# First attention's output stage: two normalisation chains laid between one another on the vector engine, the group loop written out, and the matrix engine's order rewritten to match

## The reference, cut to what matters

```python
attn_out = ctx @ out_w + out_b
h = _ln(x + attn_out, ln1_g, ln1_b)
ffn = jax.nn.gelu(h @ ffn_w1 + ffn_b1, approximate=False) @ ffn_w2 + ffn_b2
return _ln(h + ffn, ln2_g, ln2_b)
```

## Time and profile before

| | us |
|---|---|
| median of 3 runs | 3836.94 |
| the runs | 3833.84 to 3843.2 |
| the profiled execution, its own time | 3845.26 |
| its span, first to last instruction | 3843.5 |
| mean granted PE clock in it | 0.898 of full |
| the changed stage, from its first DVE operation to its last | 923.50 to 1095.64 |
| PE busy over the whole span | 3181.4 (83%) |
| DVE busy over the whole span | 2368.5 (62%) |

### The profile page before, as it was taken

How to read it: one execution, slowest core, us unless ns; L and a number is a source line. 1 busy time by engine, 2 the same in 40 slices (tenths; PEclk the granted TensorE clock), 3 DMA queues, 4 the chain that set the end, 5 groups by cost and what they waited for, 6 DMA issues and landing times. The chain is left out here.

```text
span 3843.5 us, 68233 instructions
## 1 busy us (share of the span) xinstructions
PE 3181.4 (83%) x25621; PEld 1748.6 (45%) x25621; DVE 2368.5 (62%) x5084; ACT 1844.5 (48%) x3309; POOL 921.2 (24%) x732
## 2 busy tenths in 40 slices
PE   5748888885759999797699969998888888889899
PEld 2213333331337655573222227763555444555676
DVE  5457777772656455564599942236778777778322
ACT  3214555553226423363289925434555555555444
POOL 1007888894100223000000000001121112212100
PEclk8668999997879899896599969998999988999999
DMA  4112323221033000132422210028444335432100
GB/s 146 41 51 72 106 76 103 79 91 31 12 93 132 2 1 1 45 133 79 144 58 67 68 35 1 1 81 219 122 122 101 108 103 128 122 103 82 31 9 12
DMA packets 229588, 289.46 MB, mean 75 GB/s; under 512 B 44861, under 2 KB 164121, under 8 KB 226950
## 3 DMA queue, kind: packets, MB, share of 16 engines
q1 hardware_dynamic: 229303, 285.61, 25.0%
HBM read 229.49 MB, written 56.55 MB: 74 GB/s over the span
## 5 line engine op out<-in xcount | busy, mean ns | idle before, releaser
L1169 POOL TENSOR_TENSOR l0aa_e<-l0aa_e,l0aa_et 128x512 f32<-128x512 f32 x432 | 538.1, 1274 | 139.1 <-ACT l0aa_e L1311 139.1
L2407 ACT ACTIVATE l1ba_sg<-l1ba_sg,l1ba_mn 128x128 f32<-128x128 f32 (+7 forms) x512 | 394.1, 771 | 303.4 <-DVE l1ba_mn L2451 302.4
L2451 DVE CUSTOM_DVE_ANT_0 l1ba_sg<-l1ba_pS,l1ba_tab 128x128 f32<-128x128 f32 (+7 forms) x512 | 369.0, 745 | 167.4 <-PE l1ba_pS L2347 90.1
L2347 PE MATMUL l1ba_pS<-l1b_k,l1ba_qs 64*128 64x448 f32 (+7 forms) x2048 | 372.2, 470 | 103.5 <-DMA l1ba_qs<-l1b_qd 64.9
L1342 DVE TENSOR_REDUCE l0aa_low<-l0aa_pP 128x8 f32<-128x1024 f32 x288 | 342.2, 1220 | 164.4 <-PE l0aa_pP L1193 163.6
L2460 DVE STREAM_TRANSPOSE l1ba_pT<-l1ba_sg 128x1024 f32<-128x1024 f32 (+3 forms) x344 | 367.1, 1067 | 35.7 <-PE l1ba_pO L2367 32.3
L1311 ACT ACTIVATE l0aa_e<-l0aa_pS 128x512 f32<-128x512 f32 x432 | 257.0, 595 | 259.5 <-PE l0aa_pS L1226 152.7
L2367 PE MATMUL l1ba_pO<-l1ba_pT,l1ba_v 32*64 32x256 f32 x9216 | 324.0, 397 | 5.5 <-ACT l1ba_y L2422 4.6
L319 PEld LDWEIGHTS f_pY<-l_w,f_hT 128*128 128x128 f32 x2048 | 268.1, 192 | 123.8 <-issue 118.8
L2314 POOL TENSOR_TENSOR l1ba_co<-l1ba_co,l1ba_rb 128x1024 f32<-128x1024 f32 x64 | 151.1, 2360 | 709.6 <-ACT l1ba_co L2415 676.7
L2817 ACT ACTIVATE l1aa_e<-l1aa_e 128x1536 f32<-128x1536 f32 x192 | 284.6, 1484 | 43.2 <-DVE l1aa_e L2858 25.9
(11 more groups left out here) (398 smaller groups left out, 5008.1 us busy)
## 6 DMA issues: line engine op xcount, KB each, us to landing
f_wB<-l0f_weights SPq DMA_DIRECT2D x16, 2048.0 KB, 7.2
l1ba_qs<-l1b_qd SPq DMA_DIRECT2D x128, 256.0 KB
l1ba_tab<-l1b_table SPq DMA_DIRECT2D x64, 512.0 KB
l1ba_rb<-l1b_rdd SPq DMA_DIRECT2D x64, 512.0 KB
l0aa_et<-l0a_table SPq DMA_DIRECT2D x16, 1536.0 KB
l1b_qd<-l1bp_part SPq DMA_DIRECT2D x64, 256.0 KB, 2.3
l0aa_et<-l0a_table SPq DMA_DIRECT2D x16, 512.0 KB
l0aa_qs<-l0a_qd SPq DMA_DIRECT2D x64, 96.0 KB
```

Of the source, the lines that this page charges most:

```text
L1169: nc.gpsimd.tensor_tensor(es, es, t, ALU.mult).then_inc(multiplied, 1)
L2347: ins = nc.tensor.matmul(pS[n % 2][:, at:at + half], qs[lo:lo + HALF, r % 2, i + k, :], ks[lo:lo + HALF, key:key + half], start=True, stop ...
L2407: nc.scalar.activation(row, row, ACT.Exp, bias=mn[:, r % 2, i + k:i + k + 1], scale=-1.0, accum_out=den[:, r % 2, i + k:i + k + 1]).then_i ...
L2451: nc.vector.tensor_tensor_reduce(row, scores, bias, 1.0, 3e38, ALU.add, ALU.min, mn[:, r % 2, h:h + 1]).then_inc(m_done, 1)
```

## The change

The loop over pairs of groups is gone: all engines' instructions are written out for eight groups, and register arithmetic on semaphore values falls away. On DVE the sequence is cut into pieces (`sum_B`, `projected`, `ln_newton`, `sum_A`, `apply_B`, `finish_A`, `take_sums`, `finish_B`), and in turn `g` the pieces of chain B of group g-1 stand between those of chain A of group g+1. PE's order is rewritten: `pB` of group g-1 now stands behind `pT` of group g, `pA` of g+1 ahead of the hidden tiles, `pR` of g+1 between the second and third hidden tile, `pC` of g+2 behind the fourth. Some waits are added that the new order needs (`rB_in`, `h_ready`, `a_done`, `f_in`). The arithmetic is the same.

```diff
-            def make_h(g, par):
-
-                steps = Steps(dve, stA, A_STEPS, g)
-                dve.wait_ge(cg_in[par], (g // 2 + 1) * 32)
-                dve.wait_ge(c_done, g + 1)
-                nc.vector.tensor_tensor(cT[:], cg[:, par, :], pC[:], ALU.mult).then_inc(c_in, 1)
+            def take_sums(g):
+
+                if g < GROUPS:
+                    dve.wait_ge(cg_in[g % 2], (g // 2 + 1) * 32)
+                    dve.wait_ge(c_done, g + 1)
+                    if g:
+                        dve.wait_ge(a_done, g)
+                    nc.vector.tensor_tensor(cT[:], cg[:, g % 2, :], pC[:], ALU.mult).then_inc(c_in, 1)
...
             dve.wait_ge(w_in, 16 * NW)
-            make_h(0, 0)
-            groups(dve, step)
+            take_sums(0)
+            for g in range(-1, GROUPS + 1):
+                steps_A, steps_B = Steps(dve, stA, LN_STEPS + 3, g + 1), Steps(dve, stB, LN_STEPS + 3, g - 1)
+                if g >= 1:
+                    sum_B(g - 1, steps_B)
+                if g + 1 < GROUPS:
+                    projected(g + 1)
+                if g >= 1:
+                    ln_newton(nc, dve, SB, steps_B, roughB, g)
+                if g + 1 < GROUPS:
+                    sum_A(g + 1, steps_A)
+                if g >= 1:
+                    apply_B(steps_B)
+                if g + 1 < GROUPS:
+                    finish_A(g + 1, steps_A)
+                take_sums(g + 2)
+                if g >= 1:
+                    finish_B(g - 1, steps_B)
...
-            divisors(0, 0)
+            divisors(0)
             project(0)
+            divisors(1)
             turn_back(0)
-            groups(pe, step)
+            for g in range(GROUPS):
+                turn(g)
+                if g:
+                    turn_sums(g - 1)
+                project(g + 1)
+                hidden(g, 0)
+                hidden(g, 1)
+                turn_back(g + 1)
+                hidden(g, 2)
+                hidden(g, 3)
+                divisors(g + 2)
+                back(g)
+            turn_sums(GROUPS - 1)
```

More of the change, by code:

```diff
@@ L1863, in power @@
             def power(S, ve, rough, g):
[L1864 to L1873, removed]
+                if 0 <= g < GROUPS:
+                    pool.wait_ge(ve, g + 1)
+                    nc.gpsimd.tensor_tensor(S["y"][:], S["ve"][:], C["mhalf"][:, 0:GROUP_BLOCKS], ALU.pow).then_inc(rough, 1)
+            for g in range(-1, GROUPS + 1):
+                power(SB, veB, roughB, g - 1)
+                power(SA, veA, roughA, g + 1)
         @block.vector
@@ L1889, in make_h, with statistics, projected, sum_A @@
+            def statistics(src, S, steps, ve_ready):
+                for k in range(GROUP_BLOCKS):
+                    ins = nc.vector.bn_stats(S["st"][:, k, :], src[:, k, :])
+                steps.done(ins)
+                ln_variance(nc, S, steps, ve_ready)
+            def projected(g):
                 dve.wait_ge(a_done, g + 1)
+                if g:
+                    dve.wait_ge(aB_done, g)
                 nc.vector.tensor_tensor(blocks(aT), blocks(pA), spread(ob), ALU.add).then_inc(a_in, 1)
+            def sum_A(g, steps):
@@ L1894, in make_h, with sum_B @@
                 steps.done(nc.vector.tensor_tensor(uA[:], uA[:], spread(g1), ALU.mult))
-                nc.vector.tensor_tensor(h[:, par], uA[:], spread(c1), ALU.add).then_inc(h_ready, 1)
+                if g >= 2:
+                    dve.wait_ge(rB_in, g - 1)
+                nc.vector.tensor_tensor(h[:, g % 2], uA[:], spread(c1), ALU.add).then_inc(h_ready, 1)
                 steps.close()
[L1898 to L1902, removed]
+            def sum_B(g, steps):
@@ L1938, in project, with divisors @@
-            def project(g):
-                pe.wait_ge(c_in, g + 3)
-                for k in range(GROUP_BLOCKS):
[L1941 to L1952, removed]
-                ins.then_inc(hT_done, 1)
[L1954 to L1962, removed]
+            def divisors(g):
+                if g < GROUPS:
+                    pe.wait_ge(cg_in[g % 2], (g // 2 + 1) * 32)
+                    if g:
+                        pe.wait_ge(c_in, g)
+                    nc.tensor.matmul(pC[:], sel[:], dn[:, g % 2, :], start=True, stop=True).then_inc(c_done, 1)
@@ new lines, in project, with turn_back @@
+            def project(g):
+                if g < GROUPS:
+                    pe.wait_ge(c_in, g + 1)
+                    if g:
+                        pe.wait_ge(a_in, g)
+                    for k in range(GROUP_BLOCKS):
+                        ins = nc.tensor.matmul(pA[:, k * P:(k + 1) * P], cT[:, (3 - k) * P:(4 - k) * P], ow[:], start=True, stop=True)
+                    ins.then_inc(a_done, 1)
+            def turn_back(g):
+                if g < GROUPS:
+                    pe.wait_ge(a_in, g + 1)
+                    if g:
+                        pe.wait_ge(h_ready, g)
+                    nc.tensor.matmul(pR[:], C["flip"][:], aT[:], start=True, stop=True).then_inc(aB_done, 1)
@@ L1963, in step, with back @@
+            def back(g):
+                if g:
+                    pe.wait_ge(f_in, g)
                 for t in range(FT):
```

76 lines of the change are left out of this document (48 added, 28 removed).

## The result

| us | before | changed |
|---|---|---|
| first measurement, median (lowest to highest), 5 runs each | 3836.94 (3833.84 to 3846.44) | 3812.47 (3805.96 to 3815.93) |
| second measurement, 17 and 6 runs | 3844.65 (3831.68 to 3859.51) | 3807.93 (3795.46 to 3812.67) |
| profiled execution, its span | 3843.5 | 3810.6 |
| stage, first `pC` on PE to the next stage's first product | 169.4 | 134.3 |
| stage, reciprocals to the last sum into `x` | 172.1 | 136.8 |

The ratio is 0.9928, with a 95% interval of 0.9909 to 0.9947, in the first measurement, and 0.9896 (0.9871 to 0.9921) in the second: 24.5 and 36.7 us faster. The forecast was 3806 (3797 to 3821), 31 faster, a ratio of 0.9919. Both measured times lie in that range, and both intervals hold that ratio; neither gain lies in the narrower 28 to 35 that the prediction named for its main case.

A forecast was written before the change was run, and what follows sets the result against it. A chain going back and forth between PE and DVE was taken as the bound. Turns of 13.9 instead of 18.6, with start and tail, gave 33.5 saved; less 2.5 for clock dips, 31, so 3806 us, range 3797 to 3821.

The forecast's parts named there:

- main case: Whole program: the forecast of 28 to 35 us saved, chance 0.57.
- the four waits: DVE's turn: idle 1.12 for POOL in chain B, 1.25 for `pA`, 1.35 for `pR`, 1.12 for POOL in chain A.
- The turn, 13.9: DVE's middle turn, `rB` to `rB`, in its new order: 13.9 us in place of 18.6.
- `pR` binds `rA` by 0.13: DVE's middle turn: `rA` can start only at 4.27, behind `pR`, while B's Newton step ends at 4.14.
- PE is in time, with gaps of 1.0 and 0.7, at full clock: PE's middle turn: 12.2 us of work in 13.9, so DVE binds; longest idle stretches about 1.0 and 0.7.
- The two rivals on the clock: PE's clock falls every turn, period 16.0, 18 saved, chance 0.13; or stays low throughout, 36 slower, chance 0.04.
- POOL beside DVE: POOL's power beside DVE's work: A's answer still in time, B's 0.44 later; 0 to 0.3 a turn.
- the shut-out at 1.05 a turn: Rival: A's power waits until B's gain is through; 6.3 over six turns, 27 saved, with dips 25; chance 0.18.
- The start: Stage's start: `pC` of group 1 delays `pR` of group 0 by 1.28; DVE's first full turn starts at 963.2.
- The end, 17.7 from the last `h`: Stage's tail, from the last `h` to the finished `x`: 17.7 us, where it was 20.2 with a low clock.
- The sum: Whole stage: `x` finished at 1062.1 rather than 1095.64, 33.5 earlier; 31 saved after 2.5 off for clock dips.
- The rival that the change does nothing: New order: some wait ties the chains together again, period near 18, 0 to 11 saved; chance 0.08.

## Why the prediction was right, point by point

- **What bounded it, and the four waits.** Right. They were 4.84 of 18.03; three are gone and 0.52 is left. Covering POOL's two is worth 9.6 in the stage, by the kernel that uncovers them. The prediction said that 0.9 of chain B's 1.12 would go; its own sum has DVE ready at 2.92 and the answer at 3.34, so 0.70 go. The trace has 0.60.
- **The turn, 13.9.** Measured 13.46; the term was mis-sized by 0.42, and in one way. `aT`, the application, `cT` and chain B's offset were each laid end to end behind the operation before. In the trace they start 0.08 to 0.10 before an operation ends that they don't read from: `aT` at 963.69 while the variance ends at 963.78, `h`, `cT` and the offset 0.61 and 0.59 apart with 0.69 each. That is 0.13 at `rA` (`aT` is early and so is `pR`), 0.10 behind chain A's variance and 0.19 at the turn's end. The row for it was there: in the earlier trace rows `h` starts at 981.74 and `rB` at 982.35.
- **`pR` binds `rA` by 0.13.** It does not: `rA` starts 4.14 behind `rB`, with no bracket, directly behind B's Newton step. By the 1.36 of the prediction `pR` would be there at 2.82 + 1.36 = 4.18, so it comes just in time.
- **PE is in time, with gaps of 1.0 and 0.7, at full clock.** Right: 1.15 and 1.07, clock 1.00 from 961.56 to 1028.85. The two rivals on the clock fell with that. How near they were is not known from this kernel (see the clock, at the end).
- **POOL beside DVE.** For chain B the answer comes 1.12 behind the variance (963.78 to 964.90), as before, so 0 of the 0 to 0.3. For chain A the power takes 1.03 beside four applications, 0.02 more than alone, and is over before the gain has more than begun (968.00 to 969.03; the gain starts at 968.97): the shut-out at 1.05 a turn did not occur. That the two can hold each other up is shown by the 1.38 beside a two-input product and the 1.13 of L90.
- **The start.** The full turn was to begin at 963.2; it began at 961.56, in a stage that started 0.85 earlier (reciprocals at 922.65, not 923.50), so 0.8 early.
- **The end, 17.7 from the last `h`.** Measured 1040.36 to 1059.45, 19.1: the 1.4 is the low clock in the last group's hidden tiles, the 5.31 above. It is the one dip that the allowance of 2.5 was for.
- **The sum.** 33.5 raw were expected for reciprocals to `x`, 35.3 came: 3.2 more up to the last `h`, 1.4 less behind it. Of that the spans keep 32.9; the next stage took 174.0 instead of 172.2, and 172.4 to 174.6 in the other kernels, whatever the length of the changed one.
- **The size in the whole time.** 31 expected, 24.5 and 36.7 measured. That their mean is 30.6 is luck: the stage gave 35.3, 1.8 more than the raw sum and 4.3 more than the sum with the 2.5 for dips taken off. The two measured gains lie 12 us apart, more than any term of the sum was off, so what confirms the prediction is the stage and its rows.
- **The rival that the change does nothing.** It is what each half of the change does. The prediction followed both orders together and so didn't see how far they depend on one another, nor how much the clock has to do with it (the 9.68 for 5.53 above).

## What to carry to other kernels

Where two engines pass a chain back and forth and nobody is full, lay out both engines' orders on one clock and change them together: interleaving one engine alone turned four waits of about 1.2 into one of 6.5, some 4 of which is the low clock by the estimate above. When one engine is made faster or earlier, look where its idle time moves, since the low clock moves with it. Beside a POOL operation that reads SBUF put DVE's operations with a single SBUF input, and keep the small two-input ones away from it.

## What was not expected of the hardware

- **DVE, a tiny operation that waits for a long one on POOL.** L90, 128x4 with two SBUF inputs, took 1.13 instead of 0.16 beside POOL's 1.26 sum; in the other direction POOL's power took 1.38 instead of 1.01. But a DVE product of two tiles that started 0.55 behind the start of such a power kept its 0.69. Statistics (one input) beside the same POOL sum kept their 0.87.
- **Applications beside POOL cost next to nothing.** Four TENSOR_SCALAR operations of 128x128 on fp32, SBUF to SBUF, left the power at 1.03, where it is 1.01 alone. The Trainium skill, "SBUF — State Buffer", section "Who interferes with whom", counts tensor_scalar among the operations that can enter a two-port mode and then contend; the trace shows 0.02 at most for this form. Whether the form entered that mode, no run shows.
- **DVE's starts.** Two operations that don't read one another start 0.59 to 0.61 apart at 0.69 each; with a wait on the one before it is 0.72.
- **The clock.** Turns with idle stretches of 1.15 and 1.07 kept 1.00, and so did five turns with 2.08 each, in the kernel with the gain beside POOL's power. Behind 3.51, 2.92, 2.57 and 2.41 it was low. Between these the length of the stretch does not decide: in the first kernel with the sum on POOL, PE stood 2.22 to 2.23 before `pT` four times. Three of these turns kept 1.00, and in the fourth (`pT` at 1027.17) the clock fell. The windows view has the third and a piece of the fourth:

```profile
1013.40:1027.10 13.70, 11.23 (x36) 5.19 (x36) 12.44 (x45) 4.04 (x6) 3.31 (x3) 1.00 0.00 0
1029.00:1031.00 2.00, 2.00 (x5) 1.05 (x5) 1.90 (x11) 0.00 (x0) 0.41 (x1) 0.50 0.00 0
```
